# Later scaling, casting and splitting of the output weights in a three-sub-layer decoder kernel

## The reference, cut to what matters

```python
x = x + _L0_attn_ref(_layernorm(x), Wq, Wk, Wv, Wp)
# cross-attention: 16 heads
q_big    = einsum('bshk,hkq->bshq', q_hk, w_kc_q)
q_r, k_r = einsum('bshq,hqr->bhsr', q_big, W_qr), einsum('bld,hdr->bhlr', kv_rope, W_kr)
attn     = softmax(einsum('bhsr,bhlr->bhsl', q_r, k_r))
ctx_c    = einsum('bhsl,bld->bhsd', attn, kv_rope)
ctx_lat  = einsum('bhsd,hkd->bshk', ctx_c, w_kc_kv)
out      = ctx_lat.reshape(b, s, H * K) @ Wo.T
x = x + out
x = x + _L0_ffn_ref(_layernorm(x), ...)          # routed experts, top 2 of 8
```

## Time and profile before

| | us |
|---|---|
| median of three runs | 575.76 |
| the profiled execution | 582.15 |
| its span, first to last instruction | 580.3 |
| PE busy | 536.8 (92%) |
| DVE, ACT, POOL busy | 394.6, 301.9, 295.2 |

### The profile page before, as it was taken

How to read it: one execution, slowest core, us unless ns; L and a number is a source line. 1 busy time by engine, 2 the same in 40 slices (tenths; PEclk the granted TensorE clock), 3 DMA queues, 4 the chain that set the end, 5 groups by cost and what they waited for, 6 DMA issues and landing times. The chain is left out here.

```text
span 580.3 us, 9701 instructions
## 1 busy us (share of the span) xinstructions
PE 536.8 (92%) x3449; PEld 388.4 (67%) x3449; DVE 394.6 (68%) x887; ACT 301.9 (52%) x692; POOL 295.2 (51%) x351
## 2 busy tenths in 40 slices
PE   5789999999989887699999999999999999899994
PEld 4556666766757664477777777777777776786442
DVE  5556798796677774955766557765566666786863
ACT  3064745636664675634656446666366663721430
POOL 0578742564706699960546504486035453563660
PEclk9889999999999999889999999999999999999999
DMA  8967645766442620321297324223230009225827
GB/s 239 258 231 226 212 123 178 263 197 178 167 166 88 203 73 25 85 36 46 84 240 219 78 68 121 37 36 67 45 110 1 1 2 360 105 73 109 209 92 253
DMA packets 46146, 76.98 MB, mean 133 GB/s; under 512 B 20050, under 2 KB 30068, under 8 KB 45204
## 3 DMA queue, kind: packets, MB, share of 16 engines
q1 hardware_dynamic: 42852, 63.80, 35.2%
q0 software_dynamic: 2224, 10.73, 8.4%
q10 hardware_dynamic: 1024, 1.84, 0.9%
HBM read 57.95 MB, written 28.24 MB: 149 GB/s over the span
## 5 line engine op out<-in xcount | busy, mean ns | idle before, releaser
L1974 POOL TENSOR_TENSOR xprob<-xprob,erec 128x375 f32<-128x375 f32 x112 | 92.4, 830 | 134.5 <-DVE erec L1645 134.1
L1246 ACT ACTIVATE xprob<-s_ps,nmax 128x375 f32<-128x375 f32 x112 | 64.1, 573 | 56.1 <-DVE nmax L1640 53.8
L1640 DVE TENSOR_REDUCE nmax<-s_ps 128x1 f32<-128x375 f32 x112 | 59.5, 537 | 0.2 <-PE s_ps L64 0.2
L1967 POOL TENSOR_TENSOR prob<-prob,rec 112x1792 f32<-112x1792 f32 x8 | 25.5, 3185 | 54.5 <-DVE rec L1551 54.5
L1628 DVE SCALAR_TENSOR_TENSOR pt_hl<-f_ps,pt_hl 125x384 f16<-125x384 f32 (+1 forms) x62 | 38.1, 615 | 21.4 <-ACT pt_hl L1235 20.0
L62 PE MATMUL s_ps<-kvt,qt_hl 128*128 128x376 f32 x112 | 49.4, 441 | 2.6 <-ACT xprob L1246 2.0
L62 PE MATMUL k_ps<-ow,ctx_hl 128*112 128x512 f16 x128 | 48.6, 379 | 1.4 <-DVE ctx_hl L1634 0.9
L64 PE MATMUL k_ps<-ow,ctx_hl 128*112 128x512 f16 x128 | 48.5, 379 | 0.0
L63 PE MATMUL k_ps<-ow,ctx_hl 128*112 128x512 f16 x128 | 48.5, 379 | 0.0
L1634 DVE SCALAR_TENSOR_TENSOR ctx_hl<-k_ps,ctx_hl 128x448 f16<-128x448 f32 x32 | 19.9, 623 | 38.1 <-ACT ctx_hl L1241 38.1
L63 PE MATMUL s_ps<-kvt,qt_hl 128*128 128x376 f32 x112 | 38.2, 341 | 0.0
(11 more groups left out here) (367 smaller groups left out, 1503.7 us busy)
## 6 DMA issues: line engine op xcount, KB each, us to landing
w<-w_dram SPq DMA_DIRECT2D x6, 1024.0 KB, 9.9
raw_b<-in_raw SPq DMA_DIRECT2D x8, 640.0 KB, 4.7
raw_m<-in_raw SPq DMA_DIRECT2D x8, 576.0 KB, 4.0
raw_q<-in_raw SPq DMA_DIRECT2D x8, 512.0 KB, 6.9
ow_dram<-bw_sb SPq DMA_DIRECT2D x8, 512.0 KB, 5.5
ow_raw<-ow_dram SPq DMA_DIRECT2D x8, 512.0 KB, 3.4
qw_raw<-aw_dram SPq DMA_DIRECT2D x16, 256.0 KB, 3.0
w_dram<-in_w POOLq DMA_DIRECT2D x8, 512.0 KB, 5.6
```

The costliest lines, as they stand in the source:

```text
L1246: act.activation(xprob[z][:, 0:L], s_bank(n, k)[:, 0:L], ACT.Exp, bias=nmax[:, z:z + 1], accum_out=esum[:, z:z + 1]).then_inc(xexp_done, 1)
L1640: dve.tensor_reduce(nmax[:, z:z + 1], s_bank(n, k)[:, 0:L], X, ALU.max, negate=True).then_inc(xmax_done, 1)
L1967: pool.tensor_tensor(prob[q][:, :, :, :], prob[q][:, :, :, :], rec[q][:, :, :].unsqueeze(3).broadcast_to([T, PER, GROUPS, T]), ALU.mult).t ...
L1974: pool.tensor_tensor(xprob[z][:, 0:L], xprob[z][:, 0:L], erec[:, z:z + 1].broadcast_to([128, L]), ALU.mult).then_inc(xp_ready, 1)
```

## The change

It has four parts, and no arithmetic is removed or added.

1. `most_dram` is laid out as 9 rows of 128 instead of 128 rows of 9. The store of `own_most` then goes in pieces of one number (1152 pieces of 4 bytes, before 128 of 36 bytes); the load is the same number of bytes, and DVE's maximum reads contiguous rows.
2. `find_scales` is parted: the maximum (`find_bound`) runs behind the reciprocal of tile (0,0), the six small instructions behind `pair_low(0, 3)`. Before, all stood ahead of `pair_low(0, 2)`.
3. In step 0, POOL normalises tile (0,0) before it scales pairs 0 and 1, and its two low halves move behind tiles (0,1) and (0,3). ACT's casts of pairs 0 and 1 move behind the exponentials of (0,2) and (0,3). The pairs 2 to 7 are readied by three tables, of (step, tile); before they came two a step in steps 1, 2 and 3.
4. `context_split_high` and `context_split_low` move to the end of the step, ahead of the cast and split of the gather's second half (steps 0 to 3 and 8 to 11).

```diff
-        most_dram = nc.dram_tensor("most_dram", (128, B + 1), F32).ap()
+        most_dram = nc.dram_tensor("most_dram", (B + 1, 128), F32).ap()
-        most = sb("most", [128, 128, B + 1], F32, room)
+        most = sb("most", [128, B + 1, 128], F32, room)
...
-        return (2 * n, 2 * n + 1) if 1 <= n < HALF else ()
+    SCALED = {(1, 1): 2, (1, 2): 3, (3, 0): 4, (4, 0): 5, (4, 1): 6, (5, 0): 7}
+    HIGHS = {(1, 4): 2, (1, 5): 3, (3, 2): 4, (4, 3): 5, (4, 5): 6, (5, 3): 7}
+    LOWS = {(1, 4): 2, (1, 6): 3, (3, 2): 4, (4, 3): 5, (4, 5): 6, (5, 3): 7}
...
-            sp.dma_start(most_dram, own_most[:, :]).then_inc(most_moved, 16)
+            sp.dma_start(most_dram.rearrange("b l -> l b"), own_most[:, :], allow_slow_non_contiguous=True).then_inc(most_moved, 16)
...
+                if (n, k) in HIGHS:
+                    out_weights_high(HIGHS[n, k])
...
                 for k in range(4, TILES):
                     exps(n, k)
+                context_split_high(n)
                 x_context_high(n, 1)
...
-            out_weights_high(0)
             exps(0, 0)
             pair_high(0, 3)
-            out_weights_high(1)
             x_heads_high(0, 2)
             exps(0, 1)
             exps(0, 2)
+            out_weights_high(0)
             x_heads_high(0, 3)
             exps(0, 3)
-            context_split_high(0)
+            out_weights_high(1)
             for k in range(4, TILES):
                 exps(0, k)
+            context_split_high(0)
...
+            def find_bound():
+
+                dve.wait_ge(most_moved, 32)
+                own.link(dve.tensor_reduce(bound[:, :], most[:, :, :], X, ALU.max))
+
             def find_scales():
-
-                dve.wait_ge(most_moved, 32)
-                own.link(dve.tensor_reduce(bound[:, :], most[:, :, :].rearrange("p l b -> p b l"), X, ALU.max))
...
             for k in range(4, TILES):
                 maxes(0, k)
                 recips(0, k - 1)
-                if k == 4:
-                    context_split_low(0)
             recips(0, TILES - 1)
+            context_split_low(0)
...
+            x_normalise(0, 0)
             scale_out_weights(0)
             scale_out_weights(1)
-            x_normalise(0, 0)
+            x_normalise(0, 1)
             out_weights_low(0)
-            x_normalise(0, 1)
+            x_normalise(0, 2)
+            x_normalise(0, 3)
             out_weights_low(1)
```

More of the change, by code:

```diff
@@ L499, in pair_of @@
         return 4 * (m // HALF % OCTS) + i
-    def pairs_in(n):
-        return (2 * n, 2 * n + 1) if 1 <= n < HALF else ()
+    SCALED = {(1, 1): 2, (1, 2): 3, (3, 0): 4, (4, 0): 5, (4, 1): 6, (5, 0): 7}
+    HIGHS = {(1, 4): 2, (1, 5): 3, (3, 2): 4, (4, 3): 5, (4, 5): 6, (5, 3): 7}
+    LOWS = {(1, 4): 2, (1, 6): 3, (3, 2): 4, (4, 3): 5, (4, 5): 6, (5, 3): 7}
     def kvn_count(n):
@@ L620, in _ @@
             sp.wait_ge(most_moved, 16)
-            sp.dma_start(most[:, :, :].rearrange("p l b -> p (l b)"),
-                         most_dram.rearrange("l b -> (l b)").unsqueeze(0).broadcast_to([128, 128 * (B + 1)])).then_inc(most_moved, 16)
+            sp.dma_start(most[:, :, :].rearrange("p b l -> p (b l)"),
+                         most_dram.rearrange("b l -> (b l)").unsqueeze(0).broadcast_to([128, 128 * (B + 1)])).then_inc(most_moved, 16)
             sp.wait_ge(s_done, B)
@@ L1319, in start_step @@
                 x_probs_high(n, "A", 2)
-                context_split_high(n)
                 pair_high(n, 2)
@@ L1349, in later_step @@
                     x_query_weights_high(u + 1, 2 * (s - 2))
-                for p in pairs_in(n)[0:1]:
-                    out_weights_high(p)
                 exps(n, 4)
                 x_context_high(n, 0)
-                context_split_high(n)
-                for p in pairs_in(n)[1:2]:
-                    out_weights_high(p)
                 route_part(INSIDE.get(n, ()))
@@ L1745, in start_step @@
                 x_add(n - 2)
-                context_split_low(n)
                 pair_low(n, 2)
@@ L1770, in start_step @@
                 recips(n, 6)
+                context_split_low(n)
                 x_context_low(n, 1)
@@ L1902, in _ @@
             add(ROUNDS, 0)
-            find_scales()
             pair_low(0, 2)
@@ L1908, in _ @@
             recips(0, 0)
+            find_bound()
             pair_low(0, 3)
+            find_scales()
             add(ROUNDS, 1)
@@ L2054, in _ @@
                 normalise(i, 1)
+            x_normalise(0, 0)
             scale_out_weights(0)
             scale_out_weights(1)
-            x_normalise(0, 0)
+            x_normalise(0, 1)
             out_weights_low(0)
-            x_normalise(0, 1)
+            x_normalise(0, 2)
+            x_normalise(0, 3)
             out_weights_low(1)
-            for k in range(2, TILES):
+            for k in range(4, TILES):
                 x_normalise(0, k)
@@ L2074, in _ @@
                         pool.sem_inc(norm0_ready, 1)
[L2075 to L2078, removed]
+                    if (n, k) in SCALED:
+                        scale_out_weights(SCALED[n, k])
+                    if (n, k) in LOWS:
+                        out_weights_low(LOWS[n, k])
                     if s >= 2 and k == 4:
```

## The result

The changed kernel takes 587.12 us (median of four runs, 584.75 to 591.86) beside 576.08 for the kernel before (four runs, 572.64 to 578.83): a ratio of 1.0205, 95% interval 1.0121 to 1.0289. On a second chip it was 585.65 (6 runs) beside 574.45 (17 runs), ratio 1.0191 (1.0163 to 1.0218). It is 11 us slower; I had forecast 570.9.

The account below looks back on a forecast made before the run. PE, busy 92% of the span, was taken as the bound, so only its waits could give time back. Terms -5.5 - 2.0 + 2.0 + 0.6 = -4.9 us took the median 575.76 to 570.9; range 565.5 to 577.

Parts of the forecast that it names:

- The base: The 5.90 us wait before the turned tokens and its lowered clock: 5.5 and 2.0 us gained, taken off median 575.76.
- a caution: If runs without a profile already have a shorter `r_xn` wait, part of the gain is not there; no size given.
- Step 3, first token: PE's wait for the turned tokens falls from 5.90 to 1.6 us, `r_xn` ending 0.3 behind POOL's row: 5.5 gained.
- first rival: `r_xn` gets in behind one POOL instruction and PE doesn't wait for the tokens: 1.6 us more, 569.3; chance 0.17.
- Steps 0 to 2: Moved casts and context splits delay the exponentials of (2,0) and PE's scores of (2,3): 3.85 us lost.
- The rest of step 2: From PE's scores of (2,3) to step 3, the stall goes: 4.95 us gained, net 1.1 after the 3.85 cost.
- third rival: The clock falls at PE's new waits, before the scores of (2,3) and before the tokens: 574.6; chance 0.12.
- Step 4: Casts of pairs 5 and 6 go between the exponentials of its last tiles: 2.0 us lost, lower end 0.7.
- Step 5: Pair 7's cast falls into ACT's wait for the gather: nothing lost, about 1 us if that cover were gone.
- Step 8: The context's cast moves ahead of the second gather cast, where ACT doesn't wait: 0.6 us lost.
- The store: The store in 1152 pieces takes 5 to 8 us, free up to 9.3: 0 lost, 6.1 at the upper end.
- fourth rival: The store holds up step 0, PE's first scores waiting for what exceeds 9.3 us; at 15.4, 577.0; chance 0.08.

Follow-up runs that it names:

- third trace of before: The kernel before, unchanged, profiled a third time: an execution of 575.83 us, with a short `r_xn` of 2.25 us.
- experiment 3: The changed kernel with DVE's normalised token of the end of steps 3 and 11 ahead of the context's low half again: 585.58 us, ratio 1.0106.
- Experiment 8: The changed kernel with pair 5 put into step 3 and pairs 6 and 7 into step 5, emptying step 4: 586.89 us, ratio 1.0218.

## Why the prediction was wrong

The sum failed in two ways: it subtracted a wait that about half of before's traces don't have, and it put at nothing what the moved context split, the pairs' new places in step 5 and the small-piece store cost.

- **The base (-7.5 us of the sum).** I took the 5.90 us wait and the 2.0 us of clock behind it from one execution, and the sum took them off the median too. Two of four traces of before have the long wait, and the timed runs fit the short one (argued from the table, not seen): the base was 5 us too high for all that I subtracted. The prediction had the sign of it in hand (the profiled execution lay 6.4 over the median) and named it, as "a caution", then put only some of its chance there. It should have been a rival of its own with a time: without these 5 us, 576.
- **Step 3, first token: right in size, by luck.** PE's wait was 1.02 (forecast 1.6, in the bounds 1 to 2.5), but by another mechanism than mine: `r_xn` came later, took 1.40 instead of 3 to 5, and ended with POOL's low half, not with the row, by "lock opens at the next instruction", my first rival. DVE, then POOL, in the changed kernel:

```profile
239.43 1.40 DVE L1684 TENSOR_SCALAR r_xn<-x_sb,mean,rstd 112x512 f32<-112x512 f32 x1
...
238.42 2.13 POOL L1992 TENSOR_TENSOR ow<-ow_raw,ow 128x1024 f16<-128x1024 f32 x1
240.51 1.82 POOL L1974 TENSOR_TENSOR xprob<-xprob,erec 128x375 f32<-128x375 f32 x2
```

  With the tables alone POOL has the same order there, and `r_xn` let a tile pass and ended 0.29 behind the row, as I had read it:

```profile
232.70 2.17 DVE L1682 TENSOR_SCALAR r_xn<-x_sb,mean,rstd 112x512 f32<-112x512 f32 x1
...
231.70 2.12 POOL L1990 TENSOR_TENSOR ow<-ow_raw,ow 128x1024 f16<-128x1024 f32 x1
233.78 0.80 POOL L1972 TENSOR_TENSOR xprob<-xprob,erec 128x375 f32<-128x375 f32 x1
```

  The rule of the Trainium skill, "SBUF — State Buffer", section "Who interferes with whom", is borne out by the 1.40 and by the 2.02, 2.20 and 2.25 us ones; this 2.17 and the 8.41, 8.29, 6.30, 6.18, 5.57 and 4.02 us ones are not within it. (The 8.29 is six POOL instructions, not the five that I counted.)
- **Step 3, second token, and step 11: missed.** Against the third trace of before, the changed kernel loses 2.8 from (3,6) to (4,0) and 2.4 from (11,6) to (12,0); with the token first (experiment 3) both are at most 0.1. I had put both at nothing. "In the later steps ACT waits over 1 us there", I wrote, and looked at ACT alone. On DVE the moved low half stands in front of `late_part`, whose `r_xn` PE waits for, and I had not named what is queued behind it. Experiment 3 shows it. In the table of stages the row of (4,0) falls short by 1.6.
- **Steps 0 to 2: right in kind, 1.1 short in the first trace.** 3.85 forecast, 4.95 and 3.8 in the two traces, and PE's wait at (2,3) was 1.95 where "over 2" was forecast.
- **The rest of step 2: -3.0 instead of -4.95.** The stall went. But PE, behind the new wait of 1.95, ran at 0.82 and 0.84 of the clock: 3.05 x 0.18 + 5.00 x 0.16 = 1.35 us. Experiment 8's kernel shows that this is the clock: it has the same order and the same PE wait there (1.96), but the clock stayed at 1.00, and its stretch is -4.7. This is the third rival, at one of its two places; I had argued from the earlier trace rows (0.87 at 215.53, no fall) that the clock would stay up.
- **Step 4: right** (+1.7 for 2.0). **Step 5: missed** (+1.9 for 0). "Pair 7's cast falls into ACT's wait for the gather": but from 278.08 us on POOL had two low halves, five tiles, the blank rows and a DMA issue to do with one gap of 0.30, and came to pair 7's scaling only at 287.85, 2.38 us late for ACT. I judged POOL by its busy tenths over 14.5 us, which cannot show a queue of 10 us.
- **Step 8: +1.15 for 0.6.**
- **The store: 10.8 us, not 5 to 8**, over the limit of 9.3, and 0.7 to 2.3 us lost by (0,0), where 1.5 was to be expected from the limit. The fourth rival, small.
- **A misreading ahead of the prediction**, on which no term rests: the page's line of PE's busy tenths has five slices under 9 between 160 and 250 us (8, 8, 8, 7, 6), not three.

## What to carry to other kernels

Before subtracting a long wait, look whether it repeats: a profiled execution that lies well over the median of the runs may have something in it that most of them don't (the two with the long wait lay 6.4 and 5.4 us over it, the two with the short one 1.4 and 3.5). When an instruction is moved, write out for each of its halves what stands behind it on its own engine and which engine waits for that. Work that is put into slices that look idle needs its queue counted piece by piece: pair 7's scaling came 2.4 us late in a stretch where before's page had POOL's busy tenths at 5 and 4.

## What the runs showed of the hardware

- A DVE instruction on SBUF operands alone (`r_xn` 0.53 us, the context's low half 0.60) beside a gapless row of POOL's took 1.4 to 2.3 us where it got in behind one instruction of POOL's, and 2.17, 4.02, 5.57, 6.18, 6.30, 8.29 and 8.41 where it didn't until the row had ended (0.3 to 0.4 us behind its end). In the four traces of one and the same kernel both happened twice. What decides it stays open: the starts of `r_xn` and of POOL's scaling lie within 0.11 us of each other in all four.
- A store of 4.5 KB took 2.6 to 3.3 us to land in 128 pieces of 36 bytes (ten traces), and 10.0 to 10.8 us in 1152 pieces of 4 bytes (six traces); the contiguous maximum that it buys took 1.33 us on DVE instead of 2.31.
- After a PE wait of 2.2 us in step 11 the granted clock was 1.00 in one trace of the changed kernel, 0.85 over the next full 5 us of the other, and 0.50 over 410 to 415 us with the context alone; from (11,6) to (12,0) these lost 2.4, 3.9 and 5.2 us. The same wait can cost its own length or up to 3 us more.
